# Row maxima of two heads in one double PSUM bank, and the shift turned earlier, in an attention kernel

## The reference

```python
q, k, v = (proj(Wq), proj(Wk), proj(Wv))          # [16, 16 heads, 512, 16]
q, k = _apply_rope(q, k, cos, sin)
scores = jnp.einsum('bhqd,bhkd->bhqk', q, k) / jnp.sqrt(jnp.float32(dk))
attn = jax.nn.softmax(scores, axis=-1)
out = jnp.einsum('bhqk,bhkd->bhqd', attn, v)
out = out.transpose(0, 2, 1, 3).reshape(B, S, D)
x = x + out @ Wo.T
```

## Time and profile before

| | |
|---|---|
| median of 3 runs | 2516.68 us (2516.05 to 2517.69) |
| profiled execution | 2537.58 us, span 2535.8 us |
| TensorE busy | 2269.8 us, 90% of the span |
| VectorE busy | 1696.1 us, 67% |
| ScalarE busy | 1340.0 us, 53% |
| GpSimd busy | 1138.4 us, 45% |
| mean granted TensorE clock | 0.954 of full speed |
| attention mix | about 229 to 1083 us of the span |

### The profile page before, as it was taken

One profiled execution on the slowest core, in us unless ns is written; L12 is line 12 of the kernel. 1 busy time (PEld: TensorE's weight loads), 2 busy tenths in 40 slices (PEclk: granted clock), 3 DMA queues, 4 the chain that ended last, 5 costly groups with the idle time before them and its releaser, 6 DMA issues. The chain is left out here.

```text
span 2535.8 us, 48305 instructions
## 1 busy us (share of the span) xinstructions
PE 2269.8 (90%) x14822; PEld 1238.7 (49%) x14822; DVE 1696.1 (67%) x4310; ACT 1340.0 (53%) x2741; POOL 1138.4 (45%) x1495
## 2 busy tenths in 40 slices
PE   8997788888888888889989996999999969997987
PEld 5663122222222222256556664566666646655765
DVE  7777888889888888357653333677777747763322
ACT  5765777777777777645323232555555425432322
POOL 7885111111111111034236775777777724325776
PEclk9997899999999999889989998999999989998998
DMA  6663322222213121146857884011111026675885
GB/s 199 213 206 125 76 52 71 55 75 52 70 55 75 52 69 43 37 149 203 300 163 205 215 198 69 20 37 39 36 38 35 20 72 212 229 259 163 228 213 104
DMA packets 256150, 300.01 MB, mean 118 GB/s; under 512 B 24352, under 2 KB 241648, under 8 KB 255984
## 3 DMA queue, kind: packets, MB, share of 16 engines
q1 hardware_dynamic: 222208, 249.03, 32.3%
q0 software_dynamic: 29184, 46.43, 9.0%
q10 hardware_dynamic: 4592, 2.47, 0.4%
HBM read 192.13 MB, written 105.19 MB: 117 GB/s over the span
## 5 line engine op out<-in xcount | busy, mean ns | idle before, releaser
L708 DVE TENSOR_REDUCE a_row_max<-a_ps_m 128x1 f32<-128x512 f32 x1024 | 640.7, 681 | 78.0 <-PE a_ps_m L612 67.7
L768 ACT ACTIVATE a_probs<-a_ps_s 128x512 f32<-128x512 f32 x1024 | 556.3, 598 | 234.8 <-PE a_ps_s L638 232.1
L653 PE MATMUL a_ps_o<-a_probs,a_va 128*32 128x512 f32 x2048 | 281.6, 624 | 29.3 <-ACT a_o_sb L777 28.7
L1748 POOL TENSOR_TENSOR b_spread<-b_decay,held_own_sb 128x512 f32<-128x512 f32 x256 | 267.8, 1079 | 8.6 <-DVE b_weight L1809 8.6
L1809 DVE TENSOR_TENSOR b_weight<-b_ps_s,b_spread 128x512 f32<-128x512 f32 x256 | 163.9, 683 | 9.4 <-PE b_ps_s L1950 9.4
L590 POOL DMA_DIRECT2D x<-a_xo x32 | 24.2, 755 | 276.0 <-DVE a_row_max L708 230.5
L638 PE MATMUL a_ps_s<-first_qs,first_ks 50*128 50x512 f16 x512 | 102.4, 396 | 42.1 <-ACT a_probs L768 25.4
L551 POOL CAST a_high<-a_row_max 128x32 f16<-128x32 f32 x32 | 6.5, 204 | 291.8 <-DVE a_row_max L708 291.8
L638 PE MATMUL a_ps_s<-second 50*128 50x512 f16 x512 | 102.0, 395 | 38.1 <-ACT a_probs L768 24.3
L1558 DVE SCALAR_TENSOR_TENSOR m1e_h<-m1e_act_g,m1e_xg,m1e_ps_h 128x192 f32<-128x192 f32 x64 | 26.5, 414 | 145.4 <-ACT m1e_act_g L1487 120.1
L1558 DVE SCALAR_TENSOR_TENSOR m2e_h<-m2e_act_g,m2e_xg,m2e_ps_h 128x192 f32<-128x192 f32 x64 | 26.5, 414 | 145.1 <-ACT m2e_act_g L1487 129.4
(11 more groups left out here) (397 smaller groups left out, 5380.5 us busy)
## 6 DMA issues: line engine op xcount, KB each, us to landing
parts<-second SPq DMA_DIRECT2D x16, 1536.0 KB, 6.3
rows<-m_early SPq DMA_DIRECT2D x32, 640.0 KB
m_early<-x SPq DMA_DIRECT2D x31, 512.0 KB
second<-parts SPq DMA_DIRECT2D x192, 64.0 KB
m_own<-in_L_ffn_w_gate_dram SPq DMA_DIRECT2D x24, 384.0 KB, 6.5
m_own<-in_L_ffn_w_up_dram SPq DMA_DIRECT2D x24, 384.0 KB, 6.5
m_early<-in_L_ffn_w_gate_dram SPq DMA_DIRECT2D x24, 384.0 KB, 4.9
m_early<-in_L_ffn_w_up_dram SPq DMA_DIRECT2D x24, 384.0 KB, 5.4
```

The costliest lines, as they stand in the source:

```text
L653: last = nc.tensor.matmul(ps_o[VW * j:VW * (j + 1), :], va[n.u][:, t, (h0 + j) * VW:(h0 + j + 1) * VW], probs[:, group % 2, j, t, :], star ...
L708: nc.vector.tensor_reduce(row_max[:, n.k // 4 % 2, t, e, n.p % 4:n.p % 4 + 1], m_bank(name, step)[:], AX.X, ALU.max).then_inc(m_drained, 1)
L768: nc.scalar.activation(probs[:, group % 2, j, t, :], s_bank(name, step)[:], ACT.Exp, scale=DK ** -0.5).then_inc(s_drained, 1)
L1748: nc.gpsimd.tensor_tensor(spread[:, n % 2, heads].rearrange("p h t c -> p (h t) c"), decay[:, n % 3, heads].rearrange("p h (t o) -> p (h t ...
```

## The change

The maxima of a pair's two heads go into one double bank of 2 x 512 columns, and VectorE reduces both with one instruction of 1024 columns, which gives two columns of maxima. The ring has two double banks for four single ones; shift, output and projection take a double bank each and use its first half. `M_ORDER` has four maxima turns a step for eight. The order in a step changes too. TensorE: maxima(0), scores(0), value product, shift, maxima(1), scores(1), output, and the rest as it was. VectorE: maxima(0), shift, maxima(1), normalise, maxima(2), maxima(3), residual. ScalarE: the copy of the output stands behind the two exponentials of scores(0) and no longer behind the four of scores(0) and (1). GpSimd waits for "max3", the last maxima turn of the step, as it did for "max7".

```diff
-    M_RING, S_RING = 4, 3
-    M_ORDER = ([(f"max{i}", 0, 1, 0) for i in range(4)] + [("output", L_OTURN, 2, 1), ("shift", L_TURN, 4, 3)]
-               + [(f"max{i}", 0, 1, 0) for i in range(4, 8)] + [(f"out{q}", L_OUT[q], PAIRS, PAIRS - 1) for q in range(2)])
+    M_RING, S_RING = 2, 3
+    M_ORDER = ([("max0", 0, 1, 0), ("shift", L_TURN, 4, 3), ("max1", 0, 1, 0), ("output", L_OTURN, 2, 1), ("max2", 0, 1, 0), ("max3", 0, 1, 0)] + [(f"out{q}", L_OUT[q], PAIRS, PAIRS - 1) for q in range(2)])
...
-    M_PERIOD, S_PERIOD = 2 * (8 * PAIRS + 2 + PAIRS // 2 + 2), 2 * (8 * PAIRS + 2)
+    M_PERIOD, S_PERIOD = 2 * (4 * PAIRS + 2 + PAIRS // 2 + 2), 2 * (8 * PAIRS + 2)
...
-        ps_m = [pb(f"ps_m{u}", [P, S]) for u in range(M_RING)]
+        ps_m = [pb(f"ps_m{u}", [P, 2, S]) for u in range(M_RING)]
...
-                    names = [f"max{2 * t + e}" for e in range(2)]
-                    wait(pe, m_drained, m_turn(names[1], step) + 1 - M_RING)
+                    name = f"max{t}"
+                    wait(pe, m_drained, m_turn(name, step) + 1 - M_RING)
                     for e in range(2):
                         rows = slice(EDGE * e, EDGE * e + PART_ROWS)
-                        nc.tensor.matmul(m_bank(names[e], step)[:], qs[u][rows, n.p, t * P:(t + 1) * P], ks[u][rows, n.p, :],
-                                         start=True, stop=True).then_inc(m_filled, 1)
+                        last = nc.tensor.matmul(m_bank(name, step)[:, e, :], qs[u][rows, n.p, t * P:(t + 1) * P], ks[u][rows, n.p, :],
+                                                start=True, stop=True)
+                    last.then_inc(m_filled, 1)
...
-            walk_pairs(pe, [(0, max_products(0)), (L_S, scores(0)), (L_MIX + 1, mix_values(1)), (0, max_products(1)), (L_S, scores(1)),
-                            (L_TURN, turn_shift), (L_OTURN, turn_output),
+            walk_pairs(pe, [(0, max_products(0)), (L_S, scores(0)), (L_MIX + 1, mix_values(1)), (L_TURN, turn_shift), (0, max_products(1)), (L_S, scores(1)),
+                            (L_OTURN, turn_output),
...
-                    for e in range(2):
-                        name = f"max{2 * t + e}"
-                        dve.wait_ge(m_filled, m_turn(name, step) + 1)
-                        nc.vector.tensor_reduce(row_max[:, n.k // 4 % 2, t, e, n.p % 4:n.p % 4 + 1], m_bank(name, step)[:], AX.X, ALU.max).then_inc(m_drained, 1)
+                    name = f"max{t}"
+                    dve.wait_ge(m_filled, m_turn(name, step) + 1)
+                    nc.vector.tensor_reduce(row_max[:, n.k // 4 % 2, t, :, n.p % 4], m_bank(name, step)[:], AX.X, ALU.max).then_inc(m_drained, 1)
...
-            walk_pairs(dve, [(0, maxima(0)), (0, maxima(1)), (L_OTURN, normalise), (L_TURN, copy_shift), (0, maxima(2)), (0, maxima(3)),
+            walk_pairs(dve, [(0, maxima(0)), (L_TURN, copy_shift), (0, maxima(1)), (L_OTURN, normalise), (0, maxima(2)), (0, maxima(3)),
...
-            walk_pairs(act, [(L_S, exponentials(i)) for i in range(4)] + [(L_OCOPY, copy_output)]
-                       + [(L_S, exponentials(i)) for i in range(4, 8)] + [(L_ATT[0], copy_att(0)), (L_ATT[1], copy_att(1))])
+            walk_pairs(act, [(L_S, exponentials(i)) for i in range(2)] + [(L_OCOPY, copy_output)]
+                       + [(L_S, exponentials(i)) for i in range(2, 8)] + [(L_ATT[0], copy_att(0)), (L_ATT[1], copy_att(1))])
```

More of the change, by code:

```diff
@@ L548, in split @@
                 group = n.k // 4
-                pool.wait_ge(m_drained, m_turn("max7", n) + 1)
+                pool.wait_ge(m_drained, m_turn("max3", n) + 1)
                 passed_by(pool, pool_passed)
@@ L620, in turn_shift @@
                 wait(pe, m_drained, m_turn("shift", step) + 1 - M_RING)
-                bank = m_bank("shift", step)
+                bank = m_bank("shift", step)[:, 0, :]
                 for t in range(QT):
@@ L663, in turn_output @@
                 wait(pe, m_drained, m_turn("output", step) + 1 - M_RING)
-                bank = m_bank("output", step)
+                bank = m_bank("output", step)[:, 0, :]
                 for t in range(QT):
@@ L688, in stage @@
                     wait(pe, m_drained, m_turn(f"out{q}", step) + 1 - M_RING)
-                    bank = m_bank(f"out{q}", step)
+                    bank = m_bank(f"out{q}", step)[:, 0, :]
                     for t in range(2):
@@ L717, in copy_shift @@
                 wait(dve, m_odd_loaded[f], n.base * 64 + n.k // PAIRS * 32)
-                nc.vector.tensor_copy(m_parts[:, f, :], m_bank("shift", step)[0:2 * HALF, :]).then_inc(m_drained, 1)
+                nc.vector.tensor_copy(m_parts[:, f, :], m_bank("shift", step)[0:2 * HALF, 0, :]).then_inc(m_drained, 1)
             def normalise(n, step):
@@ L724, in normalise @@
                 dve.wait_ge(m_filled, m_turn("output", step) + 1)
-                heads = m_bank("output", step)[:].rearrange("p (t j w) -> p t j w", t=QT, w=VW)
+                heads = m_bank("output", step)[:, 0, :].rearrange("p (t j w) -> p t j w", t=QT, w=VW)
                 nc.vector.reciprocal(rden[:, group % 2], heads[:, :, :, DK]).then_inc(rden_done, 1)
@@ L740, in stage @@
                     wait(dve, stored[q], n.base * 32 + n.k // PAIRS * 16)
-                    out = m_bank(f"out{q}", step)[:].rearrange("p (t d) -> p t d", d=D)
+                    out = m_bank(f"out{q}", step)[:, 0, :].rearrange("p (t d) -> p t d", d=D)
                     nc.vector.tensor_tensor(xo[:, q], out, xr[n.u][:, 2 * q:2 * q + 2, :], ALU.add).then_inc(m_drained, 1)
                 return stage
-            walk_pairs(dve, [(0, maxima(0)), (0, maxima(1)), (L_OTURN, normalise), (L_TURN, copy_shift), (0, maxima(2)), (0, maxima(3)),
+            walk_pairs(dve, [(0, maxima(0)), (L_TURN, copy_shift), (0, maxima(1)), (L_OTURN, normalise), (0, maxima(2)), (0, maxima(3)),
                              (L_OUT[0], residual(0)), (L_OUT[1], residual(1))], unrolled=2)
```

## The result

Four runs of the changed kernel: median 2492.28 us (2488.84 to 2492.82); of before on the same chip: 2517.18 (2516.05 to 2518.51). The ratio is 0.9898, interval 0.9881 to 0.9915: 24.9 us, or 1.0%, faster. The profiled execution took 2492.51 us (span 2490.8). That of before was 20.9 us above its own median, this one .2, and the two differ by 23.7 us behind the mix, where the kernels are the same. So the mix is compared by itself, and the medians only with each other.

A forecast was written before the change was run, and what follows sets the result against it. The loop of TensorE and ScalarE was taken to bound the attention mix, with VectorE beside it. Sequences -3.9, head -1.2 and clock -5 sum to -10.1 us, from 2516.7 to 2506.6 us, range 2499 to 2520.

The forecast's parts named there:

- Reduction: VectorE's merged reduction of 1024 columns: 1.21 us for 2 x .60, saving .26 us a step only if VectorE bound.
- plain step: Step without shift, output or projection: TensorE and ScalarE's loop hides the reduction's saving, gain 0, step stays 5.22 us.
- Ring: Output steps: the copy's gain (.62) nearly eaten by maxima(2)'s wait for its double bank (.51); sum -.30 us a sequence.
- Shift step: Transposes ahead of maxima(1): rows land earlier, gain .52 us across steps 0 and 1; step 4 loses .54.
- The clean sequence: One sequence of eight steps, 49.66 us before: -.26 us to 49.4, by 15 sequences -3.9 us.
- Head: Before the first scores, where VectorE does bound: 18 pairs x .065 = -1.2 us.
- The clock: Falls behind the wait for shift rows, seven sequences: shortening it to about .45 gives 0 to -7.8 us, taken as -5.
- late landings: Three late arrivals of shift rows in the 15 sequences, about 4.2 us of the extra time; not in the sum.
- 13.3 are extra: Mix's 15 sequences: 758.2 us less 744.9 at the clean period, split into half-clock first step, late landings and clock falls.
- The tail: Stage's end: the last shift's transfer bounds, so the change there is 0.
- VectorE as the bound: Rival: VectorE bounds the mix, so the whole 33 us come back, 2484 us; chance .05.
- The falls that TensorE's new waits of .5 and .4 were to bring: Rival: new waits in output and shift steps bring clock falls into the other eight sequences, +9, 2521 us; chance .07.

The follow-up runs named there:

- no wait for the rows: Kernel before, but scores leave out the two shift rows (maxima not subtracted) and the wait for them stands three steps later: 2482.73 us, ratio 0.9808.
- second profile of the full change: The changed kernel run and profiled once more, on another chip, against the kernel before on that chip: 2507.30 us, ratio 0.9913.
- the fills: Full change plus four chained small GpSimd memsets ahead of its two shift DMAs: 2646.99 us, ratio 1.0467; with SP's next-operand loads also later, 2598.49 us, ratio 1.0277.

## Why the prediction was half right

The path through the steps was right: which engine bounds, where the ring waits, what ends the wait for the scores. The sum failed in two terms, the clock's and the tail's, and these failed because of how a wait was priced.

- **Reduction.** 1.21 us forecast, 1.22 measured (four in 4.60, a pitch of 1.13 as forecast). In a plain step it changed nothing, as reckoned; VectorE had time to spare.
- **Ring.** Right, and shown from both sides. Output step: maxima(2) 3.85 forecast and 3.88 measured, value product 4.39 and 4.42, step 5.83 and 5.86. "The copy's gain (.62) is nearly eaten by the ring (.51)": the copy's move alone takes 45 us off, the merge on top of the new order gives 25 back. By the clean periods the merge costs 49.5 - 47.8 = 1.7 us a sequence. Taken from the last scores of one step to those of the next, the four output steps are .5 to .65 shorter without the merge, as much as the ring was reckoned to cost; the two shift steps are .4 and .1 longer, where VectorE begins to bound.
- **Shift step.** Right. In every second sequence the copy begins .64 behind the transposes, as forecast (671.42 and 672.06), and the next step 6.06 behind the first product (6.03). In the others it begins .80 behind, and maxima(2) stand at 3.97 (3.69) and the next step at 6.23; but the scores of step 1 stand at 6.87 (6.88), released by ScalarE, so the difference is hidden. Steps 0 and 1 together gain .55 (.57, with the .05 of their output step), and step 4 loses .43 (.54). What is short of the forecast lies in the small gains reckoned for the output steps 3 and 5, .06 and .05, which the traces do not show. The clean sequence gained .15 to .2 us instead of .26, -2.2 to -3.0 for -3.9.
- **Head.** -2.0 for -1.2. What the other .8 are wasn't looked into.
- **The clock: the step that failed.** "The term lies between 0 and -7.8 ...; I take -5" and, before it, late landings of about 4.2 us that were found and not put into the sum. Beyond the clean period 11.5 us became .4. All seven falls went, about 9 us, and one of the three late landings, about 2. So even the end of the forecast's range, -7.8, was too small: it was the rest of "13.3 are extra", and that sum is net of the first sequence, which is some 2 us shorter than the clean one. The forecast argued from the eight sequences that had the wait and no fall, that the wait is not sure to cause a fall. That holds for a single wait, and over the stage it did not matter. Where the wait is gone so are the falls (no wait for the rows: none), where it is shortened they are few (merge alone 2, shift alone 1, full change 0 and 1), and where it stays they stay (copy alone 5). The wait's price was its length and what stood beyond the clean period. The rule of the Trainium skill that the prediction weighed (TensorE: Matmul & The Clock Gate, HAM oscillation), by which the term is the whole -7.8, was nearer than -5: in the trace of after all seven falls are gone. In before the wait brought a fall in seven of 15 sequences and not in each.
- **The tail: the second.** "At the stage's end the last shift's transfer bounds: 0". The transfer still bounds, but its wait went from 3.27 to 1.96 us, and the clock, which in before had a mean of .55 over the 19 us there, is full after it. (In the second profile of the full change it falls there too, but is .59 over 4 us only.) -7.2 for 0. The fall stood in the trace of before, at the longest wait of all, and the forecast had looked for falls only between the first and the last sequence.

```profile
1033.13 0.60 PE L623 MATMUL a_ps_m<-held_ident_sb,a_high_low 128*16 128x128 f32 x4
...
1038.87 0.61 PE L638 MATMUL a_ps_s<-second 50*128 50x512 f16 x2 [3.27 <-DMA second<-a_m_parts]
```

and after:

```profile
1019.00 0.60 PE L623 MATMUL a_ps_m<-held_ident_sb,a_high_low 128*16 128x128 f32 x4
...
1024.27 0.39 PE L638 MATMUL a_ps_s<-second 50*128 50x512 f16 x2 [1.96 <-DMA second<-a_m_parts]
```

From transposes to scores these are 5.74 us in before and 5.27 in after.

- **The rivals.** VectorE as the bound would have given 2484; it is not what happened, though 2492.28 is nearer to it (8) than to the forecast (14). The reductions still wait for products, and without the merge but with the new order the time is lower, not higher. The Trainium skill's advice to keep the number of VectorE operations small (VectorE: DVE Perf Modes, Rules for kernel authors) is met with the opposite sign here: 1024 reductions of 512 columns in the new order are 25 us faster than 512 of 1024, because of the ring and not of the operations themselves. The falls that TensorE's new waits of .5 and .4 were to bring did not come.

Open: the last 2.4 us between the mix's 22.5 and the medians' 24.9; the 23.7 us by which the profiled executions differ behind the mix; how many falls before has in its unprofiled runs, of which only the mean clock is known (.956, and .965 in the full change on the same chip); why a wait of 1.3 us brings a fall in some sequences and not in others; and the cause of the occasional late landing. The median was missed by 14 us and the profiled mix by 12; the 2 between them aren't told apart.

## What to carry to other kernels

- A wait's price is its length plus what the trace shows beyond the clean period behind it, to the very end of the stage. Take the span less the number of periods times the clean period, and look at each period, since a short one hides a long one. Where a change took the wait away or made it short here, nearly the whole went: without the tail, 10.8 us became between -3.1 and 1.2, and 3.0 in the merge alone.
- One instruction for two buffers lets the first go only with the second. Time the steps where another user takes a turn of that ring: .07 us saved in each pair was paid for here with a wait of .5 in each output step.
- Do a bundle's parts apart: its best one (-45 us) was held down to -24 by another part of it, and a part that loses in one step and gains in another can be made in the one only.

## What the hardware showed unasked

- The landing of the two shift DMAs, from GpSimd's first issue to the scores that need them, was 2.35 us in most sequences of before, where the load of half a megabyte was issued .84 behind it. It was 3.7 to 4.1 when that load went .5 to .9 ahead, and mostly 4.5 to 5.4 when operand loads of 64 KB came about .5 behind it as well. So a small transfer on which an engine waits took longer where large ones of another queue had been issued before it. In both slow cases the fills stood ahead of the issue too, and before has landings of 3.6 us with the load .7 behind, so the order is not shown to be the only cause.
- Shortening a wait of 1.3 us only a little (to 1.1 in the merge alone) went with the loss of five of seven falls of the clock. Not every such wait brings a fall (one of 1.41 us in the order alone had none, nor had one of 2.52 at 988.39 in before), but where they were taken out there was none.
